# Down products of the second expert mixture as three split products

## The reference

```python
g = jnp.einsum('th,eih->eti', x, expert_gate)
u = jnp.einsum('th,eih->eti', x, expert_up)
outs = jnp.einsum('eti,ehi->eth', jax.nn.silu(g) * u, expert_down)
outs_t = jnp.transpose(outs, (1, 0, 2))
gathered = jnp.take_along_axis(outs_t, topk_idx[:, :, None], axis=1)
final = (gathered * topk_w[:, :, None]).sum(1)
shared = _mlp(residuals, shared_gate, shared_up, shared_down)
return final.reshape(orig_shape) + shared
```

## Time and profile before

| | |
|---|---|
| median of three runs | 1442.25 us (1438.18 to 1442.6) |
| profiled execution | 1442.56 us, its span 1440.7 us, mean granted clock of TensorE 0.986 |
| busy: PE, PEld, DVE, ACT, POOL | 1374.8, 1203.9, 1083.6, 863.1, 601.1 us |
| last stage, from its first instruction to the end of the last addition | 1387.55 to 1438.10 us |

### The profile page before, as it was taken

One profiled execution on the slowest core, in us unless ns is written; L12 is line 12 of the kernel. 1 busy time (PEld: TensorE's weight loads), 2 busy tenths in 40 slices (PEclk: granted clock), 3 DMA queues, 4 the chain that ended last, 5 costly groups with the idle time before them and its releaser, 6 DMA issues. The chain is left out here.

```text
span 1440.7 us, 28260 instructions
## 1 busy us (share of the span) xinstructions
PE 1374.8 (95%) x11057; PEld 1203.9 (84%) x11057; DVE 1083.6 (75%) x2162; ACT 863.1 (60%) x1706; POOL 601.1 (42%) x521
## 2 busy tenths in 40 slices
PE   8999999999999999999999999999988889999778
PEld 6888888888888888888888888888876879998558
DVE  4777887777787777787777787777896556677764
ACT  3666666666666666666666666666662236666420
POOL 4344353435353435343435343443420336766310
PEclk9999999999999999999999999999999999999889
DMA  5000000000000000000000000000025402120810
GB/s 176 1 2 27 1 27 1 27 1 27 1 27 1 27 2 27 2 27 1 27 1 27 1 3 25 2 27 2 1 77 212 149 7 91 61 73 22 351 80 4
DMA packets 11257, 59.39 MB, mean 41 GB/s; under 512 B 2346, under 2 KB 4723, under 8 KB 10100
## 3 DMA queue, kind: packets, MB, share of 16 engines
q1 hardware_dynamic: 11124, 57.59, 10.7%
HBM read 57.45 MB, written 0.13 MB: 40 GB/s over the span
## 5 line engine op out<-in xcount | busy, mean ns | idle before, releaser
L371 POOL CAST V<-Vraw 128x512 fp32r<-128x512 f32 x189 | 115.7, 612 | 575.0 <-ACT Vraw L462 575.0
L372 POOL TENSOR_TENSOR V<-Vraw,V 128x512 fp32r<-128x512 f32 x189 | 243.1, 1286 | 15.1
L672 PEld LDWEIGHTS ps<-pT,V 128*128 128x128 f32 x1568 | 214.1, 189 | 38.5 <-DVE pT L588 30.3
L672 PE MATMUL ps<-pT,V 128*128 128x256 f32 x1568 | 224.0, 282 | 20.4 <-DVE pT L588 19.7
L516 DVE TENSOR_REDUCE nmx<-ps 128x1 f32<-128x896 f32 x224 | 241.9, 1080 | 0.0
L432 ACT ACTIVATE prob<-ps,nm 128x896 f32<-128x896 f32 x224 | 222.7, 994 | 0.0
L524 DVE TENSOR_REDUCE xn<-ps 128x128 f32<-128x256 f32 x224 | 93.8, 419 | 133.2 <-PE ps L672 133.2
L462 ACT COPY Vraw<-ps 128x512 f32<-128x512 f32 x189 | 110.8, 586 | 89.9 <-PE ps L641 89.6
L423 ACT CAST Kh<-ps 128x448 fp32r<-128x448 f32 x224 | 118.9, 531 | 73.6 <-PE ps L630 73.6
L471 ACT ACTIVATE pT<-ps 128x896 fp32r<-128x896 f32 x112 | 103.1, 920 | 95.3 <-PE ps L661 93.0
L588 DVE TENSOR_TENSOR pT<-ps,pT 128x896 fp32r<-128x896 f32 x112 | 122.2, 1091 | 39.5 <-ACT pT L471 39.3
(11 more groups left out here) (325 smaller groups left out, 2554.2 us busy)
## 6 DMA issues: line engine op xcount, KB each, us to landing
raw<-in_ctxT SPq DMA_DIRECT2D x16, 896.0 KB, 4.6
d_raw<-in_ctxT SPq DMA_DIRECT2D x12, 896.0 KB, 4.7
w<-in_w SPq DMA_DIRECT2D x2, 4096.0 KB, 18.0
wg<-in_wg SPq DMA_DIRECT2D x1, 4352.0 KB, 19.4
wu<-in_wu SPq DMA_DIRECT2D x1, 4352.0 KB, 29.2
wd<-in_wd SPq DMA_DIRECT2D x1, 4352.0 KB, 39.4
e_ea<-in_alog SPq DMA_DIRECT2D x1, 2048.0 KB, 9.4
d_mrow<-in_mask SPq DMA_DIRECT2D x14, 112.0 KB, 4.5
```

What stands on the lines that cost most here:

```text
L371: link(pool, nc.gpsimd.tensor_copy(v_high(g, i), by_head(Vraw[:, j % 2, :])), "pool_chain")
L372: nc.gpsimd.tensor_tensor(v_low(g, i), by_head(Vraw[:, j % 2, :]), v_high(g, i).bitcast(F32), ALU.subtract).then_inc(sem("v_split"), 1)
L672: mm = nc.tensor.matmul(sum_of(u), V[g % 2][:, k, h % HG, :], pT[u % 2][:, k, :, :].rearrange("p a q -> p (a q)"), start=(k == 0), stop=(k ...
```

## The change

In the second mixture, the f32 down product of an expert is replaced by three fp32r products with split operands.

- Weights: GpSimd splits wd a block at a time, right behind its power: a cast into wdh and a subtraction into wdl (128x1024 each, 128x512 in the last block), two buffers. From block 2 on it waits until the down products of the block two before are done (y5_part).
- Activations: ScalarE copies act_ to acth behind each Silu (a cast), and VectorE subtracts into actl (`act_low`).
- TensorE's `down` waits for wd_split and for both halves of act_split, and issues three products for each expert.
- Three semaphores are merged to make room for new ones: wv_right and wk_right into right_split, b1_in into w1_in. The waits on w1_in now ask for both transfers.

The core of the diff:

```diff
+                def act_low(n):
+                    b, experts = n % 2, len(blocks[n])
+                    dve.wait_ge(sem("act_split"), 2 * n + 1)
+                    nc.vector.tensor_tensor(actl[b][:, 0:experts, :], act_[b][:, 0:experts, :],
+                                            acth[b][:, 0:experts, :].bitcast(F32), ALU.subtract).then_inc(sem("act_split"), 1)
...
                 link(dve, nc.vector.max(top[:, :], ch[:, :]), "mix1_chain")
+                act_low(0)
...
                 link(dve, nc.vector.tensor_reduce(one[:, 0:1], sel[:, :], AX_X, ALU.add), "mix1_chain")
+                act_low(1)
...
                     if n + 2 < len(blocks):
                         gated(n + 2)
+                        act_low(n + 2)
...
             def _(pool):
                 norm_pool(pool, 5)
+                pool.wait_ge(sem("wd_in"), 16)
+                for n, experts in enumerate(blocks):
+                    rows, high = wd[:, experts[0]:experts[-1] + 1, :], wdh[n % 2][:, 0:len(experts), :]
+                    if n >= 2:
+                        pool.wait_ge(sem("y5_part"), EB // 2 * (n - 1))
+                    link(pool, nc.gpsimd.tensor_copy(high, rows), "pool_chain")
+                    nc.gpsimd.tensor_tensor(wdl[n % 2][:, 0:len(experts), :], rows, high.bitcast(F32),
+                                            ALU.subtract).then_inc(sem("wd_split"), 1)
...
                 for n in range(len(blocks)):
                     silu(n)
+                    act.wait_ge(sem("act_ready"), n + 1)
+                    nc.scalar.copy(acth[n % 2][:, 0:len(blocks[n]), :],
+                                   act_[n % 2][:, 0:len(blocks[n]), :]).then_inc(sem("act_split"), 1)
...
                 def down(n):
-                    pe.wait_ge(sem("act_ready"), n + 1)
+                    pe.wait_ge(sem("wd_split"), n + 1)
+                    pe.wait_ge(sem("act_split"), 2 * n + 2)
                     if n >= 2:
                         pe.wait_ge(sem("y5_added"), EB * (n - 1))
                     for j, e in enumerate(blocks[n]):
-                        mm = nc.tensor.matmul(y_of(n, j), act_[n % 2][:, j, :], wd[:, e, :], start=True, stop=True)
+                        high, low, w = acth[n % 2][:, j, :], actl[n % 2][:, j, :], wdh[n % 2][:, j, :]
+                        nc.tensor.matmul(y_of(n, j), high, w, start=True, stop=False)
+                        nc.tensor.matmul(y_of(n, j), low, w, start=False, stop=False)
+                        mm = nc.tensor.matmul(y_of(n, j), high, wdl[n % 2][:, j, :], start=False, stop=True)
...
-                act.wait_ge(sem("b1_in"), 16)
+                act.wait_ge(sem("w1_in"), 32)
...
-                pe.wait_ge(sem("w1_in"), 16)
+                pe.wait_ge(sem("w1_in"), 32)
...
-                sp.dma_start(v["b1"][:, :], t["b1"]).then_inc(sem("b1_in"), 16)
+                sp.dma_start(v["b1"][:, :], t["b1"]).then_inc(sem("w1_in"), 16)
```

More of the change, by code:

```diff
@@ L352, in split_quarters, with split_weight @@
                     ins.then_inc(sem("cT_split"), 1)
-                def split_weight(w, high, low, arrived, split):
+                def split_weight(w, high, low, arrived):
                     pool.wait_ge(sem(arrived), 32)
@@ L357, in split_weight @@
                     nc.gpsimd.tensor_tensor(low[:, :, right], w[:, :, right], high[:, :, right].bitcast(F32),
-                                            ALU.subtract).then_inc(sem(split), 1)
+                                            ALU.subtract).then_inc(sem("right_split"), 1)
                 def split_values(j):
@@ L366, in split_values @@
                         pool.wait_ge(sem("wv_left"), 2)
-                        pool.wait_ge(sem("wk_right"), 1)
-                        pool.wait_ge(sem("wv_right"), 1)
+                        pool.wait_ge(sem("right_split"), 2)
                     else:
@@ L381, in _ @@
                 norm_pool(pool, 0)
-                split_weight(wv, wvh, wvl, "wv_in", "wv_right")
-                split_weight(wk, wkh, wkl, "wk_in", "wk_right")
+                split_weight(wv, wvh, wvl, "wv_in")
+                split_weight(wk, wkh, wkl, "wk_in")
                 pool.wait_ge(sem("wx_early"), 32)
@@ L718, in _ @@
                 pe.wait_ge(sem("first_vl"), 1)
-                pe.wait_ge(sem("wv_right"), 1)
+                pe.wait_ge(sem("right_split"), 1)
                 def turn(u):
@@ L739, in next_piece @@
                     if p == H0 // 2:
-                        pe.wait_ge(sem("wk_right"), 1)
+                        pe.wait_ge(sem("right_split"), 2)
                     piece(p)
@@ L842, in stage_mix1 @@
         act_ = [sb(f"f_act{i}", [P, EB, P], F32, own) for i in range(2)]
+        acth = [sb(f"f_acth{i}", [P, EB, P], F32R, own) for i in range(2)]
+        actl = [sb(f"f_actl{i}", [P, EB, P], F32R, own) for i in range(2)]
+        wdh = [sb(f"f_wdh{i}", [P, EB, D], F32R, own) for i in range(2)]
+        wdl = [sb(f"f_wdl{i}", [P, EB, D], F32R, own) for i in range(2)]
         acc = [res[:, :], sb("f_acc", [P, D], F32, own)[:, :]]
```

## The result

The changed kernel takes 1446.91 us (median of 14 runs, 1444.61 to 1449.86) beside 1443.34 for the kernel before (14 runs, 1438.18 to 1446.46). The ratio is 1.0027, with a 95% interval of 1.0017 to 1.0037: 3.6 us or 0.27% slower, and just inside the 0.3% that the prediction called no change. The profiled execution took 1447.73 us with a span of 1446.0.

A forecast was written before the change was run, and what follows sets the result against it. TensorE was taken to bound the second mixture. Terms 0.7, 0.4 to 1.0, 2.6, 0.8, 0.9 and −1.4 gave 4.3; clock +0.9 made +5.2 on 1442.56, so 1447.8 us; range 1444 to 1452 at 8 in 10.

The forecast's parts named there:

- no change: Whole kernel: a difference within about 0.3%, 4.3 us, which a measurement cannot tell from none; chance 0.35.
- slower by more: Whole kernel: slower by more than about 0.3%, 4.3 us; chance 0.62.
- Products: Second mixture's down products: 0.21 us saved a block, −1.4 for seven blocks, −1.7 in all; bounds −1.3 and −3.1.
- Step 1, xn: Stage start: GpSimd's first cast holds VectorE's xn operation (L103), making it 0.71 us later; +0.7.
- Step 2: First down block: held selection operations on VectorE delay its operands, leaving TensorE idle 0.4 to 1.0 us.
- Step 3, the gap of 2.6 us: Ahead of down(1): the rest of VectorE's selection waits for block 2's cast and subtraction; TensorE idles 2.6 us.
- Step 4: Ahead of down(2): VectorE, a block behind, has its subtraction held by GpSimd's; down(2) waits 0.8 us.
- Step 5: Later blocks: VectorE's subtraction gets in ahead of GpSimd's; 5.1 us a block, no TensorE idle time.
- The second rival: Later blocks: the loop stays caught, five more waits of 0.8, +4.0, period 5.7, 1450.5 to 1452 us; chance 0.25.
- Step 6, the tail: Last block: down(8) waits 0.95 us and the last additions start behind the last subtraction; +0.9, wait included.
- Clock: Behind the gap ahead of down(1): granted clock falls to about 0.50; about +0.9, bounds 0 to +1.9.
- First rival: Second mixture: no collision or a short one, seven blocks −1.4, tail +0.7, so −0.7, 1441.9 us; chance 0.15.

The follow-up runs named there:

- e4: Changed kernel without GpSimd's work in the second mixture, one weight pair split earlier standing in for all experts: 1440.63 us, ratio 0.9987 to the kernel before.
- e8: Changed kernel with blocks 0, 1 and the last left f32 and GpSimd starting at block 2 after the selection: 1442.26 us, ratio 0.9995 to before.
- e1: Changed kernel with six warm-up matmuls ahead of the second mixture in place of five: 1444.57 us, ratio 1.0012 to the kernel before.
- e9: Kernel before with three warm-up matmuls ahead of the second mixture in place of five: ratio 1.0018 to the kernel before.
- e5: Changed kernel with GpSimd's cast of block 2 also waiting until VectorE's selection is finished: 1444.91 us, ratio 1.0013 to the kernel before.
- e6: Changed kernel with the last block (two experts) left f32, without copy, subtraction or weight split: 1447.01 us, ratio 1.0023 to the kernel before.
- e3: Kernel before with only GpSimd's 18 split instructions added, their results read by nobody: 1445.75 us, ratio 1.0025 to the kernel before.
- e2: Changed kernel with GpSimd's first cast waiting for the second mixture's xn: 1445.90 us, ratio 1.0017 to the kernel before.

## Why the prediction was right, and where it was not

The time (1447.8 forecast, 1446.91 measured) and the main mechanism, a collision from which the loop recovers, were right. The terms were not all right, and errors of opposite sign met, so the closeness of the sum is in part luck. The price of the change was forecast as 5.2 us and came out as 4.4 in the stage and 3.6 between the medians. That is 0.27%, with an interval of 0.17 to 0.37% around the 0.3% below which the forecast spoke of no change. It had given "slower by more" 0.62 and "no change" 0.35, and the measurement doesn't decide between them.

- *Products.* The new products take 1.52 us, as computed. The saving a block is 0.30, not 0.21, in the changed kernel, in e4 and in e8. I counted the slower entry into the three-term form and not that the 32 f32 matmuls around it then take 3.48 us in place of 3.57. The seven blocks were worth −2.1, not −1.4. The Trainium skill (TensorE: Matmul & The Clock Gate, Back-to-back issue gap) gives its formula, 109 ns here, for a single matmul. In this stream of weight loads and matmuls the rows inside a block stand 119 to 120 ns apart, so it would have priced the products too low. The extra saving came from the matmuls around them. Of the bounds in the forecast, −1.3 counts the slower entry twice: 0.123 us (2.59 over 21) has it in already, and 102 products at that price save 2.1.
- *Step 1, xn.* The hold is right (1.10 us). Its price was the failing step. I put it at +0.7, and said of the clock only that it may fall behind a long gap. The hold moves the transposes by 0.46 us (2.66 into the stage in place of 2.20, since the warm-up had ended later than xn) and opens a gap of 0.24. With it TensorE stays at 1.2 GHz for 7 us more, and the other 2.8 us of down(0)'s delay come from that. e1 and e9 show it from both sides: held xn without a gap, clock up; gap without a held xn, clock down. Whether the gap itself decides or the amount of work ahead stays open.
- *Step 2.* Two operations of the selection are held (L874 to 0.70, L876 to 2.03) and down(0) does not wait, because TensorE is late itself. With the clock up (e1) it waits 0.36, at the low end of 0.4 to 1.0.
- *Step 3, the gap of 2.6 us.* The idle time is 1.12, and 1.17 with the clock up; down(1) starts 6.36 us behind down(0), 1.36 over the steady 5.00, and it is 1.36 that compares with 2.6. I let everything up to gated(1) wait for the cast and the subtraction. One operation waits for the cast (L904, and L903 in e1) and only L906, behind gated(1), for the subtraction. gated(1) has an input in PSUM, which by the earlier trace rows is not held, so it and ScalarE's copy lie beside the subtraction. I had that row and did not use it. e5 shows that the gap is this hold and no longer path.
- *Step 4.* 0.62 of idle time, or 0.86 over the steady block, for 0.8, with VectorE's subtraction held to 2.39 us as described. *Step 5.* VectorE gets ahead by 0.09 us in the next block, where I had 0.12. It stays ahead of the long one, though from then on the cast holds it to 1.05 us in three blocks, which TensorE doesn't feel. The second rival (period 5.7) falls in each of the six profiles with collisions.
- *Step 6, the tail.* down(8) waits 0.97 (0.95 forecast). To the last addition the tail is +1.23 where I had +0.9, and +1.00 to the end of the span. e6 gives 0.90 of it back. The rest stands in e6 and e8 too: VectorE's last product comes 1.24 us behind down(7) in place of 0.62.
- *Clock.* The +0.9 behind the gap ahead of down(1) did not come; the clock is 1.00 in all windows behind it.
- *First rival.* Its condition, made true in e4, gives −1.3 rather than −0.7: each product block was under-sized by 0.10, which makes 0.7 in seven, and the start is 0.1 earlier, against 0.3 more in the tail.

Sum as forecast: 0.7 + 0.7 + 2.6 + 0.8 + 0.9 − 1.4 + 0.9 = 5.2. As measured, term by term: 0.46 (xn) + 2.82 (clock at the start) + 0 (step 2) + 1.36 + 0.86 + 0 (clock behind the gap) − 7 × 0.30 + 1.00 (tail) = 4.4. So the start was 1.9 too low, and step 3 (1.2), the clock behind the gap (0.9) and the saving (0.7) were too high in cost by 2.8 together.

The rule on the lock (the Trainium skill, SBUF — State Buffer, Who interferes with whom) is borne out in this stage in both directions: L906 with two inputs in SBUF takes 1.6 us longer than before, L864 with an input in PSUM does not, and GpSimd's subtraction is the one that takes longer (2.83 in place of 2.35) when VectorE's starts first.

## What to carry to other kernels

Work given to GpSimd because it is idle is not free where VectorE runs a chain of small operations in SBUF: ask what it will start beside, and let it start behind that chain. A hold of half a microsecond may cost several, as here 0.7 cost 3.3, if TensorE's warm-up no longer reaches to its first real work; look at the granted clock of the stage's start in both traces, and make the warm-up long enough for the held case. When the earlier part of the kernel varies more than the effect, measure from the stage's own first instruction.

## What was not expected of the hardware

- A gap of 0.24 us ahead of the transposes went with a stage start that stayed at 1.2 GHz to 9.9 us, and the same warm-up without it rose within 3 us. All four kernels with that gap (the changed one, e3, e5, e6) did the former; those with xn at 0.41 us and the full warm-up, and e1 with one matmul more, did the latter.
- Idle times of 1.1 to 1.4 us ahead of a down block (the changed kernel, e1, e2), with TensorE at 2.4 GHz and busy around them, did not lower the clock.
- Where VectorE waited in this stage and two of GpSimd's instructions stood back to back, VectorE got in between. The held operations on 4 to 32 columns ended 0.02 to 0.06 us behind the first of the two, xn 0.15 us and the 128x512 subtraction 0.55 us, these two beside a next one that had nominally begun. It is no rule: in the first mixture of the kernel before, L103 began at 1129.41 beside a GpSimd instruction that ended at 1129.63, and it ended only behind the next one, the memset of the earlier trace rows.
